# A bias added on GpSimd in place of rows on TensorE, and a reordered last batch and first output, in the last two stages of a two-layer gated block

## The reference, cut to what matters

```python
x = x + tanh(g_xattn[1]) * L1_xattn(layernorm(x), ctx, ...)    # attention, then merged @ output_map
x = x + tanh(g_ffn[1]) * L1_ffn(layernorm(x), weight, bias)

def fake_quant_fp8(t):
    amax = jnp.max(jnp.abs(t))              # one maximum over the whole tensor
    scale = 448.0 / jnp.maximum(amax, 1e-12)
    q = (t * scale).astype(jnp.float8_e4m3fn).astype(jnp.float32)
    return q / scale
def L1_ffn(x, weight, bias):
    return jnp.einsum('bsd,od->bso', fake_quant_fp8(x), fake_quant_fp8(weight)) + bias
```

## Time and profile before

| | before |
|---|---|
| median of 3 runs | 1606.87 us (1606.47 to 1607.53) |
| the profiled execution | 1611.48 us, span 1609.5 us, granted clock 0.952 |
| TensorE matmul, weight load, busy | 1458.3 us (91%), 955.1 us (59%) |
| VectorE, ScalarE, GpSimd busy | 1256.9 (78%), 1021.6 (63%), 634.0 (39%) us |
| start of merge's TensorE work | 1522.20 us |
| first operation of quantise | 1574.83 us |

### The profile page before, as it was taken

The page is one execution under the profiler, slowest core; times in us unless marked ns, Lnnn a source line. Parts: engine busy times, 40 slices in busy tenths (PEclk is TensorE's granted clock), DMA queues, the critical chain, the costliest instruction groups (busy, mean ns, idle before and its releaser), DMA issues. The chain is left out here.

```text
span 1609.5 us, 29549 instructions
## 1 busy us (share of the span) xinstructions
PE 1458.3 (91%) x11053; PEld 955.1 (59%) x11054; DVE 1256.9 (78%) x2003; ACT 1021.6 (63%) x1759; POOL 634.0 (39%) x955
## 2 busy tenths in 40 slices
PE   7889999999997399999999999959979999999976
PEld 6763333333377299999999999836533333333465
DVE  6789999999765766666665564469979999999696
ACT  5538999999933344444444444426539899999636
POOL 4305555555123134344333333154415555555030
PEclk9988999999997599999999999979979999999997
DMA  8975555555263122222223221058845555566103
GB/s 275 315 228 109 127 129 126 127 123 132 73 268 112 46 66 96 66 82 97 66 82 98 66 81 46 32 177 279 257 113 125 128 127 128 127 128 128 46 0 105
DMA packets 118748, 198.65 MB, mean 123 GB/s; under 512 B 29568, under 2 KB 63680, under 8 KB 117584
## 3 DMA queue, kind: packets, MB, share of 16 engines
q1 hardware_dynamic: 83840, 111.22, 22.7%
q0 software_dynamic: 33360, 83.94, 21.0%
q10 hardware_dynamic: 1408, 1.61, 0.3%
HBM read 117.77 MB, written 77.87 MB: 122 GB/s over the span
## 5 line engine op out<-in xcount | busy, mean ns | idle before, releaser
L1142 ACT ACTIVATE i_room<-a_ring 128x512 f32<-128x512 f32 x1024 | 550.7, 605 | 61.7 <-PE a_ring L1078 14.2
L350 DVE TENSOR_REDUCE logit<-a_ring 128x2 f32<-128x1024 f32 x416 | 488.3, 1215 | 4.0 <-PE a_ring L344 3.5
L1089 PE MATMUL a_pout<-i_room,values 128*17 128x256 f32 x4096 | 309.5, 386 | 3.3 <-ACT i_room L1142 1.7
L1872 ACT ACTIVATE e_full<-e_pH,b1T 128x320 f32<-128x320 f32 x256 | 134.9, 527 | 240.8 <-PE e_pH L1813 227.1
L1821 PE MATMUL e_pY<-fc_w,e_hid_hi 128*128 128x512 f32 x640 | 237.2, 407 | 0.5 <-DVE e_hid_lo L1925 0.5
L1078 PE MATMUL a_ring<-i_qk 64*128 64x512 f32 x768 | 193.8, 502 | 19.7 <-DVE logit L350 17.1
L1638 POOL DMA_INDIRECT w<-normed,slot_get x80 | 83.8, 1048 | 248.8 <-PE fc_turned L1798 204.6
L1078 PEld LDWEIGHTS a_ring<-i_qk 64*128 64x128 f32 x768 | 72.6, 186 | 183.8 <-DVE logit L350 135.1
L1822 PE MATMUL e_pY<-fc_w,e_hid_lo 128*128 128x256 f32 x640 | 179.8, 281 | 0.0
L1089 PEld LDWEIGHTS a_pout<-i_room,values 128*17 128x17 f32 x4096 | 74.6, 95 | 175.9 <-ACT i_room L1142 137.4
L1813 PE MATMUL e_pH<-e_rowsT_hi,fc_w1T_hi 128*128 128x320 f32 x512 | 159.5, 312 | 0.0
(11 more groups left out here) (355 smaller groups left out, 2580.6 us busy)
## 6 DMA issues: line engine op xcount, KB each, us to landing
ks<-i_room SPq DMA_DIRECT2D x64, 256.0 KB, 4.0
outs<-a_osb SPq DMA_DIRECT2D x64, 256.0 KB, 3.4
qs<-i_room SPq DMA_DIRECT2D x60, 256.0 KB, 4.6
fc_raw<-in_L_ffn_fc_w SPq DMA_DIRECT2D x15, 1024.0 KB, 5.3
i_qk<-ks POOLq DMA_DIRECT2D x84, 128.0 KB, 3.4
i_qk<-qs POOLq DMA_DIRECT2D x84, 128.0 KB, 3.6
BIG<-outs SPq DMA_DIRECT2D x64, 128.0 KB
ytok<-r_zeros SPq DMA_DIRECT2D x8, 1024.0 KB, 10.3
```

Source lines behind the costliest of these rows:

```text
L350: return e.tensor_reduce(nmax[:, :].rearrange("p (x y t) -> p x y t", x=2, y=2)[:, :, p, t], pair[:, :, :], AX.X, ALU.max, negate=True)
L1089: mm = e.matmul(pout[32 * h:32 * h + VW, at], v[:, b * TPB + t, g * HG + h, :], pexp[t][:, h, at], start=(t == 0 and half == 0), stop=(t = ...
L1142: e.activation(pexp[t][:, 2 * p + hh, :], score_bank(n * U + i, hh), ACT.Exp).then_inc(exped, 1)
L1872: e.activation(full[s % 2][:, h * WIDE:(h + 1) * WIDE], pH[h][:, 0:WIDE], ACT.Silu, bias=S.b1T[:, n * KF + f:n * KF + f + 1]).then_inc(act, 1)
```

## The change

The bias row is multiplied by the gate once, on ScalarE at the start of `merge`. GpSimd then adds it to the residual: for batches 0 to 3 in `merge`, each behind `power_and_shift` of the next batch and behind ScalarE's reading of the old residual, and for batches 4 to 7 one after the other at the start of `quantise`. VectorE's outputs of batches 4 to 7 wait for theirs. The `lift` operations on VectorE and the `lifts` products on TensorE go. In the last batch of `merge` VectorE makes the variance and the shift (one fused operation), GpSimd only the power, and the maximum is taken a tile at a time. In `quantise` TensorE does output(0) ahead of turn_rounded(1). Semaphore `maxed`, which nothing waited for, goes.

```diff
--- before.py
+++ after.py
@@ -148,7 +148,7 @@
         S.logit = sb("logit", [P, NT, E])
         S.slot_get = sb("slot_get", [P, SLOTS], I32)
         S.slot_put = sb("slot_put", [P, SLOTS], I32)
-        S.amax = sb("amax", [P, B])
+        S.amax = sb("amax", [P, B - 1 + TPB])
         S.wscale, S.wrscale = sb("wscale", [P, 1]), sb("wrscale", [P, 1])
         S.wquant = sb("wquant", [P, KD, D], BF16)
 
@@ -265,9 +265,10 @@
         e.wait_ge(self.shifted, 2 * b + 1)
         e.tensor_scalar(self.shift[j][:, :], self.product[j][:, :], -1.0, None, ALU.mult).then_inc(self.shifted, 1)
 
-    def activate(self, e, b, src, dst):
+    def activate(self, e, b, src, dst, on_gpsimd=True):
         j = b % 2
-        e.wait_ge(self.shifted, 2 * b + 2)
+        if on_gpsimd:
+            e.wait_ge(self.shifted, 2 * b + 2)
         for t in range(TPB):
             e.activation(dst[:, t, :], src[:, t, :], ACT.Identity, bias=self.shift[j][:, t:t + 1],
                          scale=self.rstd[j][:, t:t + 1]).then_inc(self.normed, 1)
@@ -2225,6 +2226,14 @@
     return S.w["wk0"][:, 0, :].bitcast(BF16).rearrange("p (k o) -> p k o", k=KD)
 
 
+BIASED_EARLY = 4
+
+
+def add_bias(S, e, b):
+    x = S.X[:, tiles(b), :]
+    return e.tensor_tensor(x, x, over_tiles(S.w["fb_b"]), ALU.add)
+
+
 def merge(S):
     nc, division = S.nc, S.division
     ctx, sb, ps, sem = scope(S, "m")
@@ -2234,7 +2243,7 @@
         pY = [ps(f"pY{j}", [P, TPB, D]) for j in range(2)]
         pD = [ps(f"pD{j}", [P, SEQ]) for j in range(KD)]
         pW = ps("pW", [P, KD, D], BF16)
-        yd, upd, maxed, wtr, wte = (sem(x) for x in ("yd", "upd", "maxed", "wtr", "wte"))
+        yd, upd, late, wtr, wte = (sem(x) for x in ("yd", "upd", "late", "wtr", "wte"))
 
         with nc.Block() as block:
             @block.tensor
@@ -2266,15 +2275,24 @@
             def _(e):
                 e.wait_ge(wtr, 1)
                 e.activation(quantised_weight(S), pW[:, :, :], ACT.Copy).then_inc(wte, 1)
+                e.activation(S.w["fb_b"][:, :], S.w["fb_b"][:, :], ACT.Copy, scale=S.tg[:, 3:4])
                 for b in range(B):
-                    nb.activate(e, b, S.X[:, tiles(b), :], S.BIG[:, tiles(b), :])
+                    if b == B - 1:
+                        e.wait_ge(late, 2)
+                    nb.activate(e, b, S.X[:, tiles(b), :], S.BIG[:, tiles(b), :], b < B - 1)
                     if b == 0:
                         division.cut_high(e, LATE)
 
             @block.gpsimd
             def _(e):
-                for b in range(B):
+                for b in range(B - 1):
                     nb.power_and_shift(e, b)
+                    if 1 <= b <= BIASED_EARLY:
+                        nb.wait(e, b - 1)
+                        add_bias(S, e, b - 1)
+                nb.wait(e, B - 2)
+                e.wait_ge(late, 1)
+                e.tensor_tensor(nb.rstd[(B - 1) % 2][:, :], nb.var[(B - 1) % 2][:, :], S.half[:, :], ALU.pow).then_inc(nb.powed, 1)
 
             @block.vector
             def _(e):
@@ -2295,19 +2313,41 @@
                 def greatest(b):
                     nb.wait(e, b)
                     e.tensor_reduce(S.amax[:, b:b + 1], S.BIG[:, tiles(b), :], AX.XY, ALU.max,
-                                    apply_absolute_value=True).then_inc(maxed, 1)
-
-                for b in range(B + 1):
-                    if b < B:
-                        update(b)
-                        if b == 0:
-                            division.invert(e, LATE)
-                        if b == 1:
-                            division.cut_low(e, LATE)
-                        if b + SCALED_AHEAD < B:
-                            scale(b + SCALED_AHEAD)
+                                    apply_absolute_value=True)
+
+                def last_variance():
+                    j = (B - 1) % 2
+                    e.wait_ge(nb.agg, B * TPB)
+                    e.tensor_scalar(nb.var[j][:, :], nb.mv[j][:, :, 1], 1e-5, None, ALU.add).then_inc(late, 1)
+
+                def last_shift():
+                    j = (B - 1) % 2
+                    e.wait_ge(nb.powed, B)
+                    e.scalar_tensor_tensor(out=nb.shift[j][:, :], in0=nb.mv[j][:, :, 0], scalar=-1.0, in1=nb.rstd[j][:, :],
+                                           op0=ALU.mult, op1=ALU.mult).then_inc(late, 1)
+
+                def last_greatest():
+                    for t in range(TPB):
+                        n = (B - 1) * TPB + t
+                        e.wait_ge(nb.normed, n + 1)
+                        e.tensor_reduce(S.amax[:, B - 1 + t:B + t], S.BIG[:, n, :], AX.X, ALU.max,
+                                        apply_absolute_value=True)
+
+                for b in range(B):
+                    update(b)
+                    if b == 0:
+                        division.invert(e, LATE)
+                    if b == 1:
+                        division.cut_low(e, LATE)
+                    if b + SCALED_AHEAD < B:
+                        scale(b + SCALED_AHEAD)
+                    if b == B - 1:
+                        last_variance()
                     if b:
                         greatest(b - 1)
+                    if b == B - 1:
+                        last_shift()
+                last_greatest()
     S.division.ctx.close()
     S.inputs.ctx.close()
     S.values.ctx.close()
@@ -2322,9 +2362,6 @@
     with ctx:
         am, scale, rscale, inv1, inv = (sb(x, [P, 1]) for x in ("am", "scale", "rscale", "inv1", "inv"))
         top, kept, rec, factor, ones = sb("top", [1, 1]), sb("kept", [1, 1]), sb("rec", [1, 1]), sb("factor", [1, 1]), sb("ones", [1, P])
-        rows = 3 * 32
-        lift, rest1, rest2 = (sb(x, [rows, D]) for x in ("lift", "rest1", "rest2"))
-        lift1, lift2, lifts = (sb(x, [rows, D], BF16) for x in ("lift1", "lift2", "lifts"))
         v = [sb(f"v{j}", [P, TPB, D]) for j in range(3)]
         near, halved, half_near = ([sb(f"{x}{j}", [P, TPB, D], FP8) for j in range(3)] for x in ("near", "halved", "half_near"))
         once, twice, minus_twice = (sb(x, [P, P], FP8) for x in ("once", "twice", "minus_twice"))
@@ -2335,7 +2372,7 @@
         pY = [ps(f"pY{j}", [P, TPB, D]) for j in range(2)]
         pA, pB = pY[0][0:1, 0, 0:P], pY[1][:, 0, 0:1]
         turned, factored, oned = sem("turned"), sem("factored"), sem("oned")
-        MOST, FACTOR, SCALE, LIFTED = 1, 5, 6, 17
+        MOST, FACTOR, SCALE, INVERSE = 1, 5, 6, 9
         scaled, cut_near, cut_half, half_done, signed = (sem(x) for x in ("scaled", "cut_near", "cut_half", "half_done", "signed"))
         trv, vte, yd, fin = (sem(x) for x in ("trv", "vte", "yd", "fin"))
         st = [sem(f"st{j}") for j in range(2)]
@@ -2353,7 +2390,8 @@
             @block.gpsimd
             def _(e):
                 e.memset(ones[:, :], 1.0).then_inc(oned, 1)
-                e.memset(lifts[:, :], 0.0).then_inc(oned, 1)
+                for b in range(BIASED_EARLY, B):
+                    add_bias(S, e, b).then_inc(oned, 1)
 
             @block.scalar
             def _(e):
@@ -2409,22 +2447,23 @@
                         e.wait_ge(fin, b - 1)
                     for t in range(TPB):
                         for k in range(KD):
-                            e.matmul(pY[b % 2][:, t, :], vqT[b % 2][:, k, t * P:(t + 1) * P], wqT[:, k, :], start=(k == 0), stop=False)
-                        last = e.matmul(pY[b % 2][:, t, :], S.onesb[0:rows, :], lifts[:, :], start=False, stop=True)
+                            last = e.matmul(pY[b % 2][:, t, :], vqT[b % 2][:, k, t * P:(t + 1) * P], wqT[:, k, :], start=(k == 0),
+                                            stop=(k == KD - 1))
                     last.then_inc(yd, 1)
 
                 e.wait_ge(factored, MOST)
                 e.transpose(pA, am[:, :], S.ident[:, :]).then_inc(turned, 1)
-                e.wait_ge(oned, 2)
+                e.wait_ge(oned, 1)
                 e.wait_ge(factored, FACTOR)
                 e.matmul(pB, ones[:, :], factor[:, :], start=True, stop=True).then_inc(turned, 1)
                 e.wait_ge(signed, 3)
                 turn_rounded(0)
-                for b in range(B):
+                e.wait_ge(factored, SCALE)
+                output(0)
+                turn_rounded(1)
+                for b in range(1, B):
                     if b + 1 < B:
                         turn_rounded(b + 1)
-                    if b == 0:
-                        e.wait_ge(factored, LIFTED)
                     output(b)
 
             @block.vector
@@ -2463,32 +2502,21 @@
                 e.tensor_copy(scale[:, :], pB).then_inc(c.up(), 1)
                 e.wait_ge(c.sem, c.k)
                 e.reciprocal(rscale[:, :], scale[:, :]).then_inc(c.up(), 1)
-                e.tensor_scalar(lift[:, :], S.w["fb_b"][0:rows, :], S.wscale[0:rows, 0:1], scale[0:rows, 0:1], ALU.mult, ALU.mult).then_inc(c.up(), 1)
                 e.wait_ge(c.sem, c.k)
```

(16 more changed lines are left out.)

## The result

The changed kernel takes 1610.32 us (median of 11 runs, 1608.88 to 1611.53) against 1606.47 (11 runs, 1604.10 to 1608.48): 3.85 us slower, ratio 1.0025 with a 95% interval of 1.0016 to 1.0034. The forecast was 5.0 us slower, in a range that holds this.

The account below looks back on a forecast made before the run. ScalarE was taken to set quantise's pace, after a strict chain in merge's last batch. Terms -0.4 - 0.8 + 5.6 + 0.8 - 0.2 = +5.0 on 1606.87 gave 1611.9 us, own range 1610.5 to 1612.8, with rivals 1606.0 to 1614.1.

Parts of the forecast that it names:

- Last shift, -0.4: Last batch of merge: variance and fused shift on VectorE let ScalarE start earlier, -0.4 us.
- maxima by tile, -0.8: Last batch of merge: each tile's maximum taken while ScalarE continues, so only the last follows, -0.8 us.
- Adds in merge, 0: Merge: GpSimd's bias adds of batches 0 to 3 fit into its idle time, cost 0.
- The hold, +5.6: Start of quantise: GpSimd's four adds hold VectorE's operations ahead of turn_rounded(0), +5.6 us, bounds 0 to 6.0.
- First output ahead, +0.8: Quantise: output(0) ahead of turn_rounded(1) makes ScalarE wait before its second take_turned, +0.8 us, bounds 0.5 to 2.8.
- The other bound, 2.8: Quantise: ScalarE's wait if TensorE stays at 1.2 GHz through output(0) and turn 1; as rival +2.0, 1613.9 us, 10%.
- Rows off TensorE, -0.2: Quantise: dropping 32 bias products saves only in the tail, output 5 coming 0.15 sooner; -0.2 us.
- TensorE is not the bound: Quantise: ScalarE sets the pace, so removing 0.44 us of TensorE products a batch gains little.
- Sum, +5.0: Merge and quantise: all terms together make the changed kernel 5.0 us slower, 1611.9 us.
- VectorE gets its turn between adds: Start of quantise, rival: VectorE gets in between adds and keeps its turn; hold 3.2, sum +2.6, 1609.5 us; 20%.
- Nothing of weight is held: Start of quantise, rival: the adds leave VectorE's operations alone; sum -0.6, 1606.3 us; 15%.
- Only near(0) is held: Start of quantise, rival: only near(0) waits, for the second add; hold 0.65, 1606.9 us; 10%.

Follow-up runs that it names:

- e2: Kernel before with only the merge part: last shift on VectorE, last maxima by tile, no bias on GpSimd, quantise untouched; 1604.33 us, ratio to before 0.9992.
- e1: Changed kernel without GpSimd's four adds in quantise and the waits for them, bias of batches 4 to 7 left out; 1607.65 us, ratio to before 1.0009.
- e5: Changed kernel with each of GpSimd's four adds in quantise waiting by semaphore for the one before; 1610.38 us, ratio to before 1.0038.
- e6: Changed kernel with adds of batches 0 to 6 placed in merge, only batch 7 in quantise, new TensorE order kept; 1607.68 us, ratio to before 1.0010.
- e9: The kernel of e6, unchanged, executed once more for the clock; 1604.95 us (1 run).
- e8: Kernel before without the 32 bias products on TensorE, bias left out of the output, small VectorE operations kept; 1605.67 us, ratio to before 1.0004.
- e7: e6 with TensorE's old order, turn_rounded(1) ahead of output(0); 1604.45 us, ratio to before 0.9993.
- e4: Changed kernel with inv1 and inv fused into one VectorE tensor_scalar with one SBUF tensor; 1610.00 us, ratio to before 1.0024.
- e3: Changed kernel with TensorE's old order, turn_rounded(1) ahead of output(0); 1610.07 us, ratio to before 1.0025.
- e10: The changed kernel, unaltered, executed once more for the clock and the hold; 1611.48 us (1 run).

## Why the prediction was right, point by point

- **Last shift, -0.4, and maxima by tile, -0.8:** measured -0.44 and -0.80, and -1.25 in all; e2 has them alone. The fused 128x4 form took 0.16, the lower end of the bounds.
- **Adds in merge, 0:** right. The gap of 3.40 kept 1.07, and merge took as long up to its last mean and variance (46.97 and 46.99).
- **The hold, +5.6:** measured 5.43 (10.92 less 5.49), and e1 shows that the late adds make all of it. The mechanism was right and its course was not: I had inv1 held to the end of the second add, inv to the third, near(0) to the fourth. In fact four adds back to back let nothing in between them, and inv1 alone was held through three. Both courses end with the last add, so the size hardly changed; e5 shows that the course I drew belongs to adds with gaps. The adds took 2.31 each, not 2.4, and behind inv came 1.5 to the first turn.
- **First output ahead, +0.8:** measured 0.67 in this kernel, near the 0.5 of the full clock. That it came out so was partly luck. I had the clock rise some 3.7 after the first turn, as in rows 9; in the traces it rose 18.5 after the last mean and variance with the first turn at 15.4 (changed) as with it at 9.9 (e1). It was the hold that had moved the first turn close to the rise, and I had priced the two as independent. The other bound, 2.8, is what e1, e5, e6 and e9 paid (2.72 to 2.73). That was a rival for the changed kernel and did not happen there.
- **Rows off TensorE, -0.2:** 0.14 in the changed kernel and 0.15 in e8, up to output 5; e8's median does not move. "TensorE is not the bound" was too strong: output 5 of the kernel before stands behind TensorE's last product by 0.03, the chain from ScalarE would let it start only 0.15 sooner, and with a later clock the rows and their lift operations cost 0.69 (e2 against e7).
- **Sum, +5.0:** the trace has +4.68, the medians +3.85 with an interval of 2.6 to 5.5.
- **The rivals:** "VectorE gets its turn between adds" (+2.6) fell: 6.80 on one operation. "Nothing of weight is held" fell with the same row, and its price was wrong as well: I gave it -0.6, with 0.8 for the order, where e1, which is that case, is 1.7 above before. Without the hold the change is still slower, by its clock: e6 shows it with all of the work done (1.0001 to 1.0019). "Only near(0) is held" fell with inv1.
- **The rule of the Trainium skill** ("SBUF — State Buffer", section "Who interferes with whom") held for which operations meet: two SBUF tensors in inv1 (6.80), the tensor_scalar near(0) (6.36 in e4). Its statement that the one that issues first gets the ports fits near(0) in e5 (0.68, the add behind it 2.74) and not the ties of rows 7, and does not tell what happens to one that waits behind a queue; the rows do.

## What to carry to other kernels

Before moving work to GpSimd, list what VectorE runs meanwhile: reductions, PSUM reads and single elements passed here, while a two-SBUF-tensor operation on one column waited through three adds. The same adds cost next to nothing (0.05) when each stood beside such harmless work (e6, e7). And a reordering that puts an idle stretch into TensorE's first work at 1.2 GHz is to be priced at both clocks: here the same swap cost 0.67 or 2.73 by when the clock rose. And a gain ahead of such a start can shrink, since the rise need not come sooner with the work: of e2's 1.24 us some 0.7 was left by output 5.

## What the runs showed of the hardware that I had not expected

Four GpSimd adds back to back did not let a waiting VectorE operation in (6.80 through three adds), but with a semaphore wait between them they did (e5: 0.16, 2.24, 0.68, 2.83, 2.83 on VectorE, and 10.33 for the adds in place of 9.23). A one-input tensor_scalar on 128x1 inside an add took 0.27 and passed (e4).

TensorE's granted clock rose 3.1 us after the first turn in the changed kernel and 8.5 after it in e1 and e6, where the same sequence ran: some 2.7 busy, 1.2 idle, then busy. Counted from the end of the last mean and variance, it is one moment for these three:

| | first turn | clock rises |
|---|---|---|
| changed, e3, e4, e10 | 15.1 to 15.4 | 18.45 to 18.57 |
| e1, e6, e9 (new order) | 9.9 to 10.0 | 18.50 to 18.51 |
| e2, e7 (old order) | 9.9 to 10.0 | 15.11 to 15.12 |
| before (old order) | 11.2 | 15.05 |
| e5 (new order) | 13.0 | 21.97 |
| e8 (old order) | 11.2 | 13.98 |

In e8 merge itself took 45.29 up to that mark, where all others have 46.97 to 46.99. With the first turn at 9.9 to 10.0 the order on TensorE goes with the moment of the rise (e6 against e7); with the order alike (changed and e1) 5.4 us of first turn did not move it. Why it comes at these moments no run here settles.
